# The last expert layer of a decoder: rows sorted by expert into whole tiles instead of every expert over every row

## The reference, cut to what matters

```python
x = hidden_states.reshape(-1, d)                    # 2048 x 128, after layernorm
logits = jnp.einsum('td,ed->te', x, router_w)       # 8 experts
top_logit, top_idx = jnp.max(logits, axis=-1), jnp.argmax(logits, axis=-1)
score = jax.nn.sigmoid(top_logit)
onehot = jax.nn.one_hot(top_idx, n_experts, dtype=x.dtype)
xs = x * score[:, None]
g = jnp.einsum('td,edf->etf', xs, expert_gate)      # f = 256
u = jnp.einsum('td,edf->etf', xs, expert_up)
h = jax.nn.silu(g) * u
eo = jnp.einsum('etf,efd->etd', h, expert_down)
moe_out = jnp.einsum('te,etd->td', onehot, eo)
sh = jax.nn.silu(x @ shared_gate) * (x @ shared_up) @ shared_down
return (moe_out + sh).reshape(seq, bs, d)           # added to the residual x
```

## Time and profile before

| | us |
|---|---|
| median of 3 runs | 2006.76 (2005.99 to 2008.98) |
| the profiled execution | 2005.79 |
| its span | 2004.1 |
| TensorE busy | 1633.5 (82%) |
| VectorE busy | 908.0 (45%) |
| ScalarE busy | 714.0 (36%) |
| GpSimd busy | 438.4 (22%) |

### The profile page before, as it was taken

The page is one execution under the profiler, slowest core; times in us unless marked ns, Lnnn a source line. Parts: engine busy times, 40 slices in busy tenths (PEclk is TensorE's granted clock), DMA queues, the critical chain, the costliest instruction groups (busy, mean ns, idle before and its releaser), DMA issues. The chain is left out here.

```text
span 2004.1 us, 31793 instructions
## 1 busy us (share of the span) xinstructions
PE 1633.5 (82%) x11656; PEld 953.8 (48%) x11656; DVE 908.0 (45%) x2506; ACT 714.0 (36%) x1434; POOL 438.4 (22%) x517
## 2 busy tenths in 40 slices
PE   6899889975799998869889997317157999959998
PEld 4343434434444444545634445306033555548887
DVE  4555255523355564551245644502465555224443
ACT  2344323342277675514213344202132433322221
POOL 5432243300211101000045310050543443000000
PEclk9999999998999998969989998659577999969999
DMA  7000000000000000000040000023100000000000
GB/s 222 6 1 1 1 1 2 1 1 0 1 1 1 1 1 1 1 1 1 1 155 2 1 1 1 2 67 83 38 11 11 8 10 7 1 0 0 0 0 21
DMA packets 37725, 33.44 MB, mean 17 GB/s; under 512 B 3956, under 2 KB 31832, under 8 KB 37592
## 3 DMA queue, kind: packets, MB, share of 16 engines
q1 hardware_dynamic: 33728, 26.65, 4.4%
q0 software_dynamic: 2048, 4.20, 0.7%
q10 hardware_dynamic: 1816, 0.81, 0.2%
HBM read 23.26 MB, written 8.39 MB: 16 GB/s over the span
## 5 line engine op out<-in xcount | busy, mean ns | idle before, releaser
L1324 ACT ACTIVATE scores_L_experts_L<-L3x_psL 128x512 f32<-128x512 f32 x128 | 76.4, 597 | 173.3 <-PE L3x_psL L1187 169.7
L1361 DVE CUSTOM_DVE_ANT_0 L3x_junk<-L3x_psS,L3x_mask_rows 128x256 f32<-128x256 f32 x224 | 86.2, 422 | 92.1 <-PE L3x_psS L1149 84.0
L2448 ACT ACTIVATE L3f_activated<-L3f_psG 128x512 f32<-128x512 f32 x72 | 43.0, 597 | 153.0 <-PE L3f_psU L2427 153.0
L2481 DVE TENSOR_TENSOR L3f_hidden<-L3f_activated,L3f_psU 128x512 f32<-128x512 f32 x72 | 49.6, 688 | 103.0 <-ACT L3f_activated L2448 103.0
L1187 PE MATMUL L3x_psL<-identb,L3x_mask_parts 128*128 128x256 bf16 x768 | 95.8, 275 | 0.0
L867 ACT ACTIVATE L0x_probs<-L0x_psL 128x512 f32<-128x512 f32 x96 | 52.1, 594 | 114.2 <-PE L0x_psL L680 79.0
L867 ACT ACTIVATE L2a_probs<-L2a_psL 128x512 f32<-128x512 f32 x96 | 52.1, 594 | 107.3 <-PE L2a_psL L678 72.5
L867 ACT ACTIVATE L0a_probs<-L0a_psL 128x512 f32<-128x512 f32 x96 | 52.1, 594 | 102.3 <-PE L0a_psL L678 66.5
L1169 PE MATMUL L3x_psL<-L3x_qm,ctx_T 32*128 32x512 f32 x256 | 73.1, 645 | 12.5 <-DVE L3x_mx L1361 11.6
L2413 PE MATMUL L3f_psY<-experts_L_L,L3f_hidden 128*128 128x128 f32 x576 | 77.2, 277 | 5.0 <-DVE L3f_hidden L2481 4.9
L1187 PEld LDWEIGHTS L3x_psL<-identb,L3x_mask_parts 128*128 128x128 bf16 x768 | 70.3, 98 | 21.4 <-issue 13.7
(11 more groups left out here) (762 smaller groups left out, 3992.7 us busy)
## 6 DMA issues: line engine op xcount, KB each, us to landing
packed_rows<-zeros SPq DMA_DIRECT2D x1, 2560.0 KB, 21.4
L2f_rows<-packed_rows SPq DMA_DIRECT2D x8, 320.0 KB, 3.6
unpacked_rows<-L2f_y SPq DMA_DIRECT2D x8, 320.0 KB, 2.7
experts_L_L<-in_L_ffn_w_dram SPq DMA_DIRECT2D x1, 2048.0 KB, 8.7
scores_L_experts_L<-in_L_ffn_w_dram SPq DMA_DIRECT2D x1, 2048.0 KB, 8.2
L3x_mask_rows<-in_mask_Bx1xSxS_ff_dram SPq DMA_DIRECT2D x8, 256.0 KB, 2.7
experts_L_L<-n_L_ffn_expert_gate_dram SPq DMA_DIRECT2D x1, 1024.0 KB, 13.6
experts_L_L<-in_L_ffn_expert_up_dram SPq DMA_DIRECT2D x1, 1024.0 KB, 6.8
```

Of the source, the lines that this page charges most:

```text
L1324: nc.scalar.activation(probs[:, half, a, k, :], psL[i % RING][:], ACT.Exp).then_inc(s_prob, 1)
L1361: last = nc.vector.tensor_tensor_reduce(out=junk[:, i, :], in0=psS[a][:, i * S:(i + 1) * S], in1=mrow[:, b % 2, t, :], scale=1.0, scalar=L ...
L2481: nc.vector.tensor_tensor(hid[:, j % 2, g[0]:g[0] + n, :], act_out[:, u % 2, 0:n, :], psU[u % 2][:, 0:n * S].rearrange("p (c s) -> p c s", ...
```

## The change

The four blocks become two: `turn_and_route` stays, and the new `one_expert` does the rest, the output's store included.

VectorE finds the one-hot choice. TensorE counts by two matmuls how many rows of an expert lie earlier within a tile and in each whole tile, and VectorE sums these over the tiles by doubling shifts, rounds each expert's number of rows up to a multiple of 128 and sums over the experts. This gives each row a slot. The slots fill at most 16 + 7 = 23 tiles of 128 rows, each of one expert alone, and the kernel always runs all 23. GpSimd scatters the scaled rows to their slots in `packed_rows` by 16 indirect DMAs, SyncE loads the 23 tiles back in six groups, TensorE turns them. For each tile GpSimd reads the offset of its expert's weights into a register (`value_load`) and copies these weights, 768 elements per partition, from `experts_L1_L3` into a ring of three buffers, from which the matmuls read. A tile has 4 matmuls up, SiLU, product, and 2 down. ScalarE copies each group's output out of PSUM, SyncE stores it to `unpacked_rows`, and when all are stored GpSimd gathers the rows by 16 indirect DMAs; VectorE adds them in four chunks, and each chunk is stored to the output when ready.

The shared expert runs over the rows in their first order, in four chunks of 512, between the ranking and the reload. On TensorE its first four matmuls stand ahead of the two rank matmuls. The weights of an expert now lie side by side (gate, up, down), so that one copy takes them all. The load of the down weights becomes two DMAs. The prologue gets one iota and one copy more, for the tiles' first row numbers.

```diff
@@ load_and_turn, last_experts
+  steps.step(nc.gpsimd.iota(w["tile_int"][:], pattern=[[P, NT + 7]], base=0, channel_multiplier=0))
+  steps.step(nc.vector.tensor_copy(w["tile_at"][:], w["tile_int"][:]))
-  (w["L3_ffn_down"][:, 0:8, :, :], dram["L3_ffn_expert_down"].rearrange("e (c f) d -> f e c d", f=P)),
+  (w["L3_ffn_down"][:, 0:8, 0, :], dram["L3_ffn_expert_down"].rearrange("e (c f) d -> f e c d", f=P)[:, :, 0, :]),
+  (w["L3_ffn_down"][:, 0:8, 1, :], dram["L3_ffn_expert_down"].rearrange("e (c f) d -> f e c d", f=P)[:, :, 1, :]),
@@ turn_scaled, route_top1: removed whole
...
@@ one_expert (new, indentation reduced)
+def one_expert(nc, mem, w, name, hT, h_all, logits, packed, unpacked, out, E):
+  CHUNK = 4
+  CHUNKS = NT // CHUNK
+  WIDE = CHUNK * P
+  TILES = NT + E - 1
+  GROUPS = (TILES + CHUNK - 1) // CHUNK
...
+  RING = 3
...
+  ONE = every.shape[1] // (E + 1)
...
+  mine = sb("weights", [P, RING, ONE])
...
+# GpSimd
+  pool.wait_ge(s_slot, 1)
+  for t in range(NT):
+    if t % CHUNK == 0:
+      pool.wait_ge(s_scaled, t // CHUNK + 1)
+    nc.gpsimd.indirect_dma_start(packed, bass.IndirectOffsetOnAxis(ap=slot[:, t:t + 1], axis=0),
+                  h_all[:, t, :], None).then_inc(s_scatter, 16)
+  pool.wait_ge(s_offset, 1)
+  for i in range(TILES):
+    at = pool.value_load(offset[0:1, i:i + 1], min_val=0, max_val=(E - 1) * ONE)
+    if i >= RING:
+      pool.wait_ge(s_tdown, i - RING + 1)
+    nc.gpsimd.tensor_copy(mine[:, i % RING, :], every[:, bass.ds(at, ONE)]).then_inc(s_mine, 1)
+  pool.wait_ge(s_store, 16 * GROUPS)
+  for t in range(NT):
+    nc.gpsimd.indirect_dma_start(back_rows[:, t, :], None, unpacked,
+                  bass.IndirectOffsetOnAxis(ap=slot[:, t:t + 1], axis=0)).then_inc(backs[t // CHUNK], 16)
...
+# SyncE
+  sp.wait_ge(s_scatter, 16 * NT)
+  for j in range(GROUPS):
+    sp.dma_start(xe[:, group(j)[0]:group(j)[-1] + 1, :], rows_of(packed, j)).then_inc(s_load[j], 16)
+  for j in range(GROUPS):
+    sp.wait_ge(s_y, j + 1)
+    sp.dma_start(rows_of(unpacked, j), y[:, group(j)[0]:group(j)[-1] + 1, :]).then_inc(s_store, 16)
...
+  for c in range(CHUNKS):
+    sp.wait_ge(s_x, c + 1)
+    at = slice(c * CHUNK, (c + 1) * CHUNK)
+    sp.dma_start(final[:, at, :], mem.x[:, at, :]).then_inc(s_out, 16)
+  sp.wait_ge(s_out, 16 * CHUNKS)
...
+# TensorE
+  def shared_up(c):
+    for f in range(PARTS):
+      if c >= 1:
+        pe.wait_ge(s_hid, PARTS * (c - 1) + f + 1)
+      nc.tensor.matmul(psG[f][:], common[:, f * P:(f + 1) * P], hT[:, c * WIDE:(c + 1) * WIDE], start=True, stop=True)
+      nc.tensor.matmul(psU[f][:], common[:, UP + f * P:UP + (f + 1) * P], hT[:, c * WIDE:(c + 1) * WIDE], start=True, stop=True).then_inc(s_up, 1)
...
+  def turn(j):
+    pe.wait_ge(s_load[j], 16)
+    if j >= 1:
+      pe.wait_ge(s_xT, j)
+    for k, i in enumerate(group(j)):
+      last = nc.tensor.transpose(psX[:, k * P:(k + 1) * P], xe[:, i, :], mem.ident[:])
+    last.then_inc(s_turned, 1)
+  def tile_up(i):
+    j, k = divmod(i, CHUNK)
+    pe.wait_ge(s_xT, j + 1)
+    if i < 2:
+      pe.wait_ge(s_hid, PARTS * CHUNKS)
+    else:
+      pe.wait_ge(s_thid, i - 1)
+    pe.wait_ge(s_mine, i + 1)
+    rows, own = xT[:, j % 2, k * P:(k + 1) * P], mine[:, i % RING, :]
+    for f in range(PARTS):
+      nc.tensor.matmul(psG[i % 2][:, f * P:(f + 1) * P], own[:, f * P:(f + 1) * P], rows, start=True, stop=True)
+    for f in range(PARTS):
+      last = nc.tensor.matmul(psU[i % 2][:, f * P:(f + 1) * P], own[:, UP + f * P:UP + (f + 1) * P], rows, start=True, stop=True)
+    last.then_inc(s_tup, 1)
+  def tile_down(i):
+    j, k = divmod(i, CHUNK)
+    pe.wait_ge(s_thid, i + 1)
+    if k == 0:
+      if j >= 2:
+        pe.wait_ge(s_y, j - 1)
+      else:
+        pe.wait_ge(s_add, CHUNKS)
+    for f in range(PARTS):
+      last = nc.tensor.matmul(psY[j % 2][:, k * D:(k + 1) * D], hid[:, i % 2, 0, f * P:(f + 1) * P],
+                  mine[:, i % RING, DOWN + f * D:DOWN + (f + 1) * D], start=f == 0, stop=f == PARTS - 1)
+    last.then_inc(s_tdown, 1)
...
+  shared_up(0)
+  pe.wait_ge(s_one, 1)
+  nc.tensor.matmul(psR[:, 0:NT * E], w["earlier"][:], one[:], start=True, stop=True)
+  nc.tensor.matmul(psR[:, NT * E:2 * NT * E], w["ones"][:], one[:], start=True, stop=True).then_inc(s_ranked, 1)
+  for c in range(1, CHUNKS + 1):
+    if c < CHUNKS:
+      shared_up(c)
+    shared_down(c - 1)
+  turn(0)
+  for i in range(TILES + 1):
+    if i < TILES:
+      if i % CHUNK == 0 and down_group(i) + 1 < GROUPS:
+        turn(down_group(i) + 1)
+      tile_up(i)
+    if i >= 1:
+      tile_down(i - 1)
...
+# ScalarE
+  act.wait_ge(chain, 1)
+  nc.scalar.activation(score[:], top[:, :, 0], ACT.Exp, scale=-1.0).then_inc(e_done, 1)
...
+  for c in range(CHUNKS):
+    for f in range(PARTS):
+      u = PARTS * c + f
+      act.wait_ge(s_up, u + 1)
+      if u >= 2:
+        act.wait_ge(s_hid, u - 1)
+      nc.scalar.activation(act_out[:, f, :], psG[f][:], ACT.Silu).then_inc(s_act, 1)
+  for i in range(TILES + 1):
+    if i < TILES:
+      act.wait_ge(s_tup, i + 1)
+      if i < 2:
+        act.wait_ge(s_hid, PARTS * CHUNKS)
+      else:
+        act.wait_ge(s_thid, i - 1)
+      nc.scalar.activation(act_out[:, i % 2, 0:FF], psG[i % 2][:, 0:FF], ACT.Silu).then_inc(s_tact, 1)
+    if i >= 1 and (i % CHUNK == 0 or i == TILES):
+      j = (i - 1) // CHUNK
...
+      act.wait_ge(s_tdown, i)
+      nc.scalar.copy(y[:, g[0]:g[-1] + 1, :], psY[j % 2][:, 0:len(g) * D].rearrange("p (t d) -> p t d", d=D)).then_inc(s_y, 1)
...
+# VectorE
...
+  def keep_rows(j):
+    dve.wait_ge(s_turned, j + 1)
+    if j >= 2:
+      dve.wait_ge(s_tup, CHUNK * (j - 1))
+    n = len(group(j)) * P
+    nc.vector.tensor_copy(xT[:, j % 2, 0:n], psX[:, 0:n]).then_inc(s_xT, 1)
+  def tile_hidden(i):
+    dve.wait_ge(s_tact, i + 1)
+    if i >= 2:
+      dve.wait_ge(s_tdown, i - 1)
+    else:
+      dve.wait_ge(s_down, CHUNKS)
+    nc.vector.tensor_tensor(hid[:, i % 2, 0, 0:FF], act_out[:, i % 2, 0:FF], psU[i % 2][:, 0:FF], ALU.mult).then_inc(s_thid, 1)
+  first_best(nc, steps, w, logits[:], top[:], equal[:], key[:], one[:], E)
+  dve.sem_inc(s_one, 1)
...
+  dve.wait_ge(e_done, 1)
+  steps.step(nc.vector.tensor_scalar(score[:], score[:], 1.0, None, ALU.add))
+  steps.step(nc.vector.reciprocal(score[:], score[:]))
+  dve.wait_ge(s_ranked, 1)
...
+  steps.step(nc.vector.tensor_copy(before[0][:, 8:8 + NT, :], counts))
+  for n, shift in enumerate(SHIFTS):
...
+    steps.step(nc.vector.tensor_tensor(new[:, 8:8 + NT, :], old[:, 8:8 + NT, :], old[:, 8 - shift:8 + NT - shift, :], ALU.add))
...
+  steps.step(nc.vector.tensor_scalar(used[:], ahead[:, 7 + NT:8 + NT, :], float(P - 1), None, ALU.add))
+  steps.step(nc.vector.tensor_scalar(used[:], used[:], -P, None, ALU.bitwise_and))
+  steps.step(nc.vector.tensor_copy(ends[0][:, :, 4:4 + E], used[:]))
+  for n, shift in enumerate(SHIFTS[0:3]):
...
+    steps.step(nc.vector.tensor_tensor(new[:, :, 4:4 + E], old[:, :, 4:4 + E], old[:, :, 4 - shift:4 + E - shift], ALU.add))
...
+  steps.step(nc.vector.tensor_tensor(equal[:], ahead[:, 7:7 + NT, :], psR[:, 0:NT * E].rearrange("p (t e) -> p t e", e=E), ALU.add))
+  steps.step(nc.vector.tensor_tensor(equal[:], equal[:], starts.to_broadcast(wide), ALU.add))
+  steps.step(nc.vector.tensor_tensor(equal[:], equal[:], one[:], ALU.mult))
+  steps.step(nc.vector.tensor_reduce(rank[:], equal[:], AX.X, ALU.add))
+  nc.vector.tensor_copy(slot[:], rank[:, :, 0]).then_inc(s_slot, 1)
+  for c in range(CHUNKS):
+    at = slice(c * CHUNK, (c + 1) * CHUNK)
+    nc.vector.tensor_tensor(h_all[:, at, :], h_all[:, at, :], score[:, at].unsqueeze(2).to_broadcast([P, CHUNK, D]),
+                ALU.mult).then_inc(s_scaled, 1)
+  steps.step(nc.vector.tensor_tensor(past[:], w["tile_at"][:].unsqueeze(2).to_broadcast([P, TILES, E]),
+                   stops.to_broadcast([P, TILES, E]), ALU.is_ge))
+  steps.step(nc.vector.tensor_reduce(expert[:], past[:], AX.X, ALU.add))
+  nc.vector.tensor_scalar(offset[:], expert[:, :, 0], float(E - 1), float(ONE), ALU.min, ALU.mult).then_inc(s_offset, 1)
+  for c in range(CHUNKS + 1):
+    if c < CHUNKS:
+      shared_hidden(c)
+    if c >= 1:
+      shared_add(c - 1)
+  keep_rows(0)
+  for i in range(TILES):
+    if i % CHUNK == 0 and i // CHUNK + 1 < GROUPS:
+      keep_rows(i // CHUNK + 1)
+    tile_hidden(i)
+  for c in range(CHUNKS):
+    at = slice(c * CHUNK, (c + 1) * CHUNK)
+    dve.wait_ge(backs[c], 16 * CHUNK)
+    dve.wait_ge(s_add, c + 1)
+    nc.vector.tensor_tensor(mem.x[:, at, :], mem.x[:, at, :], back_rows[:, at, :], ALU.add).then_inc(s_x, 1)
@@ decoder
+  w["L3_experts"] = shared[:, 0:9 * 3 * 256]
+  nine = w["L3_experts"].rearrange("p (e f) -> p e f", e=9)
+  w["L3_ffn_gate"], w["L3_ffn_up"] = nine[:, :, 0:256], nine[:, :, 256:512]
+  w["L3_ffn_down"] = nine[:, :, 512:768].rearrange("p e (c d) -> p e c d", c=2)
+  w["tile_at"], w["tile_int"] = sb("tile_at", [P, NT + 7]), sb("tile_int", [P, NT + 7], I32)
```

(12 more changed lines are left out.)

130 lines of the change are left out of this document (80 added, 50 removed).

## The result

The changed kernel takes 1886.93 us (median of 4 runs, 1883.85 to 1888.33) where the kernel before took 2006.51 beside it: 0.940 of the time, interval 0.9383 to 0.9416. The forecast was 1887.9. The profiled execution took 1888.33, its span is 1886.5; it is the slowest of the four.

What follows compares the result with a forecast made beforehand. It took TensorE's matmuls of all eight experts over all rows as the bound. Rebuilding the stage from 1780.73 step by step ended the span at 1885.2 instead of 2004.1, giving a median of 1887.9 us; 80% range 1877 to 1915.

Steps and rivals of the forecast that it cites:

- What bounds the kernel, and what goes: Last expert stage: TensorE's matmuls of eight experts over all rows bound it; 217.1 us from logits to last add are replaced.
- Choosing and ranking: From the logits to the first scatter: counts at 1787.5, 16 VectorE steps of 4.3 us, slots 1791.8, GpSimd begins 1792.8.
- Scatter: Sixteen indirect DMAs 1.27 us apart take 20.0, plus 0.1 for VectorE's scalings; end at 1812.9.
- Shared expert, costed at nothing: Beside scatter and reload: TensorE's work ends at 1815.3, before sorted tiles could start at 1817.5, a cover of 2 us.
- Back into SBUF: Reload after the last scatter: TensorE starts at 1817.5, tile 0 goes up at 1819.6, the other loads land ahead of use.
- The 23 tiles: Sorted tiles: TensorE 1.41 and GpSimd 1.38 us per tile, level, so 1.5 with stalls; 34.5 in all, to 1854.1.
- rival 1: Sorted tiles: TensorE alone sets the pace, 1.41 us per tile, reads and copies hidden; 2.1 less, down to 1882; chance 0.22.
- Gather, add, store: After the tiles: first gather 1859.6 after a 3.3 us wait, gathers 1.26 apart, last add ends 1881.85, output ends 1885.0.
- The sum: Whole kernel: span ends at 1885.2 in place of 2004.1, 118.9 us less; median 1887.9.
- Rival 2: Sorted tiles: slow register reads with nothing running ahead, 2.0 to 3.6 us per tile, result 1899 to 1936; chance 0.19.
- Rival 3: TensorE's clock stays lower through the shared expert, 14 us late, 1902; through the tiles too, 1932; chance 0.07.
- Rival 4: Sorted tiles: GpSimd pays a long switch from each register read to copy; slower than before above 6.7 us per tile; chance 0.02.

Runs made afterwards that it cites:

- the kernel with the pause: Changed kernel, with TensorE beginning the shared expert's fourth chunk only after VectorE has added the second; 1884.2 us, 0.9388.
- three chunks: Changed kernel, with three shared expert chunks beside the scatter and the fourth moved behind the sorted tiles; 1883.8 us, 0.9383.
- two copies: Changed kernel, with GpSimd copying each tile's weights a second time, to a buffer nobody reads; 1891.1 us, 0.9425.
- the kernel kept warm: Changed kernel with fourth chunk behind the tiles and rank matmuls ahead of the shared expert, plus 9 unread matmuls before the first turn; 1880.9 us, 0.9376.
- fixed offset: Changed kernel, with the weight copies taking a constant offset in place of the register read per tile; 1889.1 us, 0.942.
- rank first: Changed kernel, with the two rank matmuls ahead of the shared expert's first four matmuls on TensorE; 1885.4 us, 0.9394.
- half of the scatter: Changed kernel, with only the first 8 of 16 tiles scattered and waited for; 1880.3 us, one run.
- the last kernel: Changed kernel with a wait before the fourth chunk and rank matmuls first, plus ScalarE scaling the rows and 3 unread matmuls before the first turn; 1880.70 us, 0.9377.

## Why the prediction was right, and where it was right by luck

**What bounds the kernel, and what goes.** Right: the stretch after the logits fell from 223.4 to 105.9, and 104.5 were forecast.

**Choosing and ranking.** Right within 0.3 at the slots. The nine wide steps took 0.325 each and the small ones 0.2, as taken (1787.74 to 1791.88). Of the eight records ahead of the rank matmuls five ran at the lower clock (0.85 each) and three at the higher (0.43), where four and four were assumed; that is 0.4, and the counts came 0.3 late. The first scatter waited 0.5 longer than I had it.

**Scatter.** Right: 1.27 each, except that the first takes 1.36 and the second comes 1.67 after it. Where ScalarE had scaled the rows beforehand, the first took 1.10 and the second came 1.41 after it, so some 0.25 may be the cost of VectorE's scalings beside the first; the forecast had 0.1 for it. From the third scatter on no row shows a cost by VectorE or TensorE.

**Shared expert, costed at nothing.** Wrong in its outcome in the changed kernel's two traces, by something that stood in none of the rivals. The work of TensorE itself is as summed: at +20.1 of the scatter (33.0 after the logits) its records were through but for the last down-projection. The hold-up then brought the shared expert's end to 41.2 instead of 34.6, past the cover of 2 us. Since the reload's limit is 24.35 after the first scatter, it cost 28.2 - 24.35 = 3.8 at the first turn. In the kernel with the pause, without a hold-up, the shared expert ended 22.96 after the first scatter, 1.4 inside that limit, though it had waited 0.78 more: costed at nothing was right there.

**Back into SBUF.** Right: 24.7 after the first scatter forecast, 24.35 in the kernels without a hold-up.

**The 23 tiles.** The term of the sum that was mis-sized on the other side: 36.1 forecast, 34.2 measured. Tile 0 up to the end of the last down-projection but one took 33.0, that is 23 x 1.43 where 23 x 1.5 stood, and the last tile's tail 1.2 where 1.6 stood. It is rival 1's mechanism that runs. GpSimd's copies, in the changed kernel, wait for TensorE; its rows in the view by line, from 1823 to 1861:

```profile
L3089 POOL COPY L3f_weights<-experts_L_L 128x768 f32 x20 | 16.6, 829 | 22.5 <-PE L3f_psY L3162 22.5
```

20 copies, 16.6 us busy, and 22.5 us of idle time, all of it ended by TensorE's down-projection. The copy was right (0.83), but two numbers around it were not: the gap (0.77 from one to the next, where I had 0.88) and the register read (nothing, where I had 0.5 between bounds of 0 and 2.7; the 2.7 was the landing of a store of 320 KB, not of a small one). So GpSimd's pace is 0.77, not 1.38, and it is not level with TensorE. TensorE's own pace is 1.45 (19 intervals of the copies, 1826.89 to 1854.46), where I had 1.41. I had taken 1.5 for both engines with stalls. Rival 1 had 1.41 and a total near 1882; less the hold-up's 3.8 the median would be 1883.1, and the kernels with three chunks or a pause have 1883.8 and 1884.2, between rival 1 and the forecast. The read's price of about 600 ns, which the Trainium skill's page "DMA: Bandwidth & Descriptors", section "Latency and other measured facts", gives for a tensor load, can't be seen here: the interval of 0.77 is the same with a read in it and without. What that section says of the load itself may hold if the load runs beside the copy before it.

**Gather, add, store.** The gathers took 18.8 as summed, add and output 6.6 for 6.7. From the last copy to the first gather it took 2.3 where L2f's 3.3 was taken over: 1.0 too much.

**The sum.** +0.8 to the first scatter, +3.5 to the first turn (the hold-up), +0.3 for the turn, -1.9 in the tiles, -1.1 from the last tile to the first gather and -0.2 in small terms make the +1.4. The forecast time is right, and by luck so near: the deviations above and below are 4.6 and 3.2, and they cancelled in the main. The median is nearer still, 1.0 under the forecast, because the profiled execution lies 1.4 above the median, where the forecast put it 1.0 below.

**The rivals.** Rival 2 (slow reads) is out by the kernel with two copies. Rival 3 (the lower clock) is true in part: the clock was at 0.5 from 0.9 ahead of the first scatter to 5.9 behind it, with the shared expert's first 3.4 us there, and again from +23 to +30 or +33, around the first turn. Against the kernel kept warm, turn and tiles are 0.4 longer in the changed kernel's first trace and 1.7 in its second; a wait of 7.7 us ahead of the turn cost 1.8. The Trainium skill's warning that gaps return the array to half rate ("TensorE: Matmul & The Clock Gate", section "HAM oscillation — how this bites in real kernels") agrees with these rows: 0.50 in the 5.3 us after a wait of 7.71 us, 1.00 with matmuls in its place. I had the rule and gave it no term at the first turn. Rival 4 didn't happen: GpSimd's first copy began with the end of its last scatter (1813.80).

**What stays open.** What holds TensorE's results back, and whether it happens in executions whose recording is complete. Shown: the hold-up stood in all five traces with missing events (the changed kernel twice, fixed offset, two copies, rank first) and in none of the eight complete ones. In three of the five ScalarE took up the fourth chunk at 22.4 to 22.6 after the first scatter; with the fixed offset and with two copies it took up the first half at +21.0 and the second at +22.4, and VectorE's add came at +18.8. All this ended about 1 us after the last scatter had landed. The eight others have half of the scatter, three chunks or none, or a wait of 0.78 us, but not one of them was traced with missing events, nor the changed kernel without; so whether it was an edit or the kind of the execution that ended the hold-up no run tells. Against the edits speaks that the two groups part in L2f, 400 us ahead, and in this stage at +7: up to there all 64 events of the scatter are in every trace, and of the 192 that follow, 50 to 61 are in the five and all in the others with the whole scatter, while half of the scatter, three chunks and the pause differ from the changed kernel only from +10, +14.7 and +14.9 on. Nor is it the chip alone: the last kernel ran on the same one as four of the five, and its trace is complete.

The missing events by themselves are no late signals. From +7 to +13.9 the five traces have 4 to 6 of the 11 signals between TensorE, ScalarE and VectorE, and in four of the five ScalarE and VectorE began on their work at the same places as in the trace of the pause within 0.1 us; in the first trace the two halves of chunk 2 came 1.1 and 0.8 late. So signals came that were not recorded. The late ones behind +15 may be a delay of the chip that befell some executions, or one that the recording itself brought about; every time here comes from an execution whose span is recorded, so no run tells these apart. The medians go the same way as the traces (0.9383 and 0.9388 without the hold-up, 0.940 and 0.9412 with it), but their intervals overlap. The changed kernel traced until one trace of it is complete, or the kernel with the pause until one is not, would decide between edit and execution.

## What to carry to other kernels

Give a transfer or a helper engine its price per instruction from a row in which such instructions follow each other, not from one's duration; and look for register reads behind the instruction before them, where they cost nothing as long as that one runs. Work that is "hidden" beside a chain of transfers needs its own event in the forecast (when is it over, and what starts then), since that is where this forecast missed most. Before an edit gets the credit for what is gone from a trace, look whether the two traces are alike ahead of the edit's place, in their number of events too. And compare two versions of a late stage by its stretch in the trace, from a fixed event on, when what lies ahead of it varies by more than the edit is worth.

## What the runs showed of the hardware

- TensorE's results reached their consumers 4 to 8 us late beside 16 indirect scatters, in the five traces of the changed stage that lack 317 to 341 of the 512 landing events of L2f's gathers, and in none of the eight that have them all. The cause is open.
- The recording can lose more than half of the events while the engines keep their time: from +7 to +13.9 of the scatter 32 to 39 landing events are left where the trace of the pause has 89, and in four of these five traces ScalarE and VectorE were within 0.1 us of that trace.
- A read of a register from SBUF on GpSimd adds nothing between two copies of 768 elements, which follow 0.77 apart while each is recorded with 0.83.
- Indirect gathers of 128 rows are 1.25 apart, but single ones take 1.41 to 1.47 instead of 0.95: none in some traces (18.8 us for 16), one in others (19.3), three in one (20.3).
- After a wait of 1.46 us in front of the first turn, the granted clock was at its lower level for 3.4 us of the following tiles; in the last kernel, with three matmuls in that place and the scaling moved, it stayed up, and turn and tiles were 1.3 shorter.
